# A four-layer graph network on one core: set-up work becomes steps in the ordered list of group steps, and split signals become whole ones

## What is computed

```python
h = relu(layernorm(x)); x = x + L0(h, adj)   # attention whose softmax runs over rows, plus h @ self_weight
h = relu(layernorm(x)); x = x + L1(h, adj)   # GAT, layernorm, relu, sum over (adj + (1+eps) I), MLP with a layernorm
h = relu(layernorm(x)); x = x + L2(h, adj)   # GAT with elu
h = relu(layernorm(x)); x = x + L3(h, adj)   # learned matrix A: off-diagonal and diagonal parts, two weights
...
def L1(x, adj):
    h = x @ Wp + bp
    scores = leaky_relu(s_src[:, :, None] + s_dst[:, None, :])
    attn = softmax(where(adj > 0, scores, fill), axis=-1)
    h_gat = relu(layernorm((attn * adj) @ h, gat_g, gat_b))
    z = relu(layernorm(((1 + eps) * h_gat + adj @ h_gat) @ W1 + b1, mlp_g, mlp_b))
    return relu(z @ W2 + b2 + h_gat)
...
def L3(x, adj, W, e, bias):        # e: values of the nonzero entries, in order of rows
    A = softmax(where(adj > 0, e[rank of the entry], NEG), axis=1)
    return (A off its diagonal) @ (x @ W[1]) + (its diagonal) * (x @ W[0]) + bias
```

## Time and profile before

| | |
|---|---|
| median of 3 runs | 968.9 us (968.21 to 969.45) |
| the profiled execution | 968.08 us, of which its span 966.3 us |
| PE busy | 906.3 us (94%) |
| PE weight loads busy | 857.2 us (89%) |
| DVE busy | 833.4 us (86%) |
| ACT busy | 757.8 us (78%) |
| POOL busy | 426.2 us (44%) |
| mean granted TensorE clock | 0.987 |

### The profile page before, as it was taken

How to read it: one execution, slowest core, us unless ns; L and a number is a source line. 1 busy time by engine, 2 the same in 40 slices (tenths; PEclk the granted TensorE clock), 3 DMA queues, 4 the chain that set the end, 5 groups by cost and what they waited for, 6 DMA issues and landing times. The chain is left out here.

```text
span 966.3 us, 21073 instructions
## 1 busy us (share of the span) xinstructions
PE 906.3 (94%) x7027; PEld 857.2 (89%) x7027; DVE 833.4 (86%) x2593; ACT 757.8 (78%) x2048; POOL 426.2 (44%) x1123
## 2 busy tenths in 40 slices
PE   4868899999998899999999999999999999998998
PEld 4668798999898899999989989989999999988997
DVE  5779899999869989988889989789999879789983
ACT  4698768877778887796887788898768787679953
POOL 6553326533546533362643454644353445244330
PEclk9889999999999999999999999999999999999999
DMA  5200000000020010011000101100100100000003
GB/s 139 66 2 2 2 2 1 1 2 1 23 65 3 1 45 1 2 44 45 1 2 1 45 2 45 44 2 1 45 1 2 46 1 2 22 2 1 1 2 110
DMA packets 43052, 20.05 MB, mean 21 GB/s; under 512 B 8248, under 2 KB 42432, under 8 KB 42944
## 3 DMA queue, kind: packets, MB, share of 16 engines
q1 hardware_dynamic: 41056, 18.49, 7.1%
q10 hardware_dynamic: 1888, 0.21, 0.2%
HBM read 10.17 MB, written 8.39 MB: 19 GB/s over the span
## 5 line engine op out<-in xcount | busy, mean ns | idle before, releaser
L729 PE MATMUL ps<-HE,PT 128*128 128x129 f32 x2048 | 239.4, 276 | 6.8 <-issue 4.4
L729 PEld LDWEIGHTS ps<-HE,PT 128*128 128x128 f32 x2048 | 233.2, 192 | 9.7 <-issue 6.7
L498 ACT ACTIVATE Y<-X,SM 128x128 f32<-128x128 f32 x512 | 204.1, 491 | 19.5 <-POOL SM L494 18.9
L479 POOL TENSOR_TENSOR SM<-ST 128x8 f32<-128x8 f32 x96 | 26.0, 271 | 380.5 <-DVE ST L1300 380.5
L1444 DVE SCALAR_TENSOR_TENSOR PT<-ps,CE,maskT 128x512 f32<-128x512 f32 x256 | 174.2, 743 | 16.8 <-PE ps L849 12.6
L490 POOL TENSOR_TENSOR SM<-SM,minus_half 128x8 f32<-128x8 f32 x96 | 163.6, 1704 | 7.6
L729 PE MATMUL ps<-W,HT 128*128 128x128 f32 x768 | 117.1, 275 | 0.1
L729 PEld LDWEIGHTS ps<-W,HT 128*128 128x128 f32 x768 | 106.1, 192 | 4.0 <-issue 0.7
L1300 DVE BATCH_NORM_STATS2 ST<-X 128x6 f32<-128x128 f32 x512 | 105.0, 278 | 3.4
L1075 ACT ACTIVATE HE<-ps,HE 128x128 f32<-128x128 f32 x256 | 68.9, 379 | 0.0
L748 PE MATMUL ps<-ident,Y 128*128 128x128 f32 x512 | 67.9, 276 | 1.0 <-ACT Y L498 0.6
(11 more groups left out here) (263 smaller groups left out, 2274.5 us busy)
## 6 DMA issues: line engine op xcount, KB each, us to landing
X<-in_x_dram SPq DMA_DIRECT2D x32, 256.0 KB, 3.5
out_dram<-X SPq DMA_DIRECT2D x32, 256.0 KB, 2.7
adj_raw<-in_adj_dram SPq DMA_DIRECT2D x4, 256.0 KB, 3.7
UP<-US SPq DMA_DIRECT2D x64, 2.0 KB, 1.8
W<-in_L_gnn_W_dram SPq DMA_DIRECT2D x2, 64.0 KB, 3.9
W<-in_L_gnn_W_dram SPq DMA_DIRECT2D x1, 128.0 KB, 3.6
feat0w<-L_gnn_others_weight_dram ACTq DMA_DIRECT2D x1, 64.0 KB, 3.3
feat1w<-in_L_gnn_Wp_dram ACTq DMA_DIRECT2D x1, 64.0 KB, 3.7
```

The costliest lines, as they stand in the source:

```text
L479: TT(sm[:, S_DIF, :], st[:, :, 1], st[:, :, 4], ALU.subtract)
L498: a = nc.scalar.activation(dst[:, n, 0:F], src[:, n, 0:F], func, scale=SM[s][:, S_RSTD, n:n + 1], bias=SM[s][:, S_SHIFT, n:n + 1])
L729: return nc.tensor.matmul(o, w, m, start=start, stop=stop, skip_group_check=True)
```

## The change

The first block is gone. Its constants, loads, transposes, and the copies of `maskT` and of the turned weights stand at the top of each engine's stream in the one block that is left; the rest became steps of group "g": `counts`, `masks`, `vecs` (DVE), `offs` (PE, ACT), `rows_b` (ACT), `offc` (PE, DVE), `biases` (POOL). The meeting of all engines is replaced by waits inside the steps that need a result: `made["vec"]` in PE's `feat0` and ACT's `norm0` of the first three groups, `made["bias"]` in ACT's `norm0`, PE's `feat1` and DVE's `shift3`, `made["masks"]` in `coefp0`, `coefb0`, `self0`, `made["counts"]` in `coefb0`. `egin` and `elow` move to the end of the list.

The loads are dealt out anew: `adj` pieces 0 and 2 on SP's queue, 1 and 3 on ACT's, where they stand ahead of the three weight matrices (`TURNED`) and of the seven columns that are left in `WEIGHTS`; `VECTORS` shrink from eleven DMAs to seven and go to SP's queue. DVE makes `adjn` piece by piece, waits for all of `WEIGHTS`, and then goes on to `counts`.

`scaled` signals once after all eight rows; so do `split0`, `splitb0`, `low0`, `lowb0`. `agg0` finishes one tile after the other. `TURNS` and `HOMES` are new strings.

DVE now begins with `counts`, 0:`stat0`, `masks`, `vecs`, `offc`, `erow`, 1:`stat0`, 2:`stat0`, `eat`, 4:`stat0`, 0:`feat0`. PE: `offs`, `offc`, `erank`, `eoffm`, 0:`norm0`, `eedge`, 1:`norm0`, 0:`feat0`, 1:`feat0`, `ecover`, `evalue`, 2:`norm0`, 2:`feat0`, 0:`cmax0`, 4:`norm0`, 1:`cmax0`, 0:`coefb0`, 1:`coefb0`, `eturn`, 0:`agg0`. ACT: `offs`, `rows_b`, `erank`, 0:`scale0`, 1:`scale0`, `eedge`, 0:`norm0`, 1:`norm0`, 0:`feat0`, `eat`, 1:`feat0`, 2:`scale0`, `emask`, 2:`norm0`, 2:`feat0`, 4:`scale0`, 0:`cmax0`, `esoft`, 1:`cmax0`, `escale`, 0:`split0`, 0:`splitb0`. POOL: 0:`stat0`, 1:`stat0`, `biases`, `egin`, 2:`stat0`, 4:`stat0`. Up to 0:`agg0` PE had the same steps before in another order, but for 4:`feat0` where there is now 2:`feat0`.

At the end, PE has f:`att2a`, c:`norm3`, f:`att2b`, c:`agg3`, e:`norm3`, e:`agg3`, c:`feat3`, d:`feat3`, f:`norm3`, f:`agg3`, e:`feat3`, f:`feat3`, where it had f:`att2a`, f:`att2b`, d:`norm3`, c:`feat3`, e:`norm3`, d:`agg3`, e:`agg3`, d:`feat3`, f:`norm3`, f:`agg3`, e:`feat3`, f:`feat3`. DVE has f:`elu2b`, e:`low3`, b:`shift3`, e:`shift3`, f:`elu2`, f:`stat3`, b:`feat3`, f:`low3`, where it had f:`elu2b`, d:`shift3`, f:`elu2`, f:`stat3`, e:`low3`, e:`shift3`, b:`feat3`, f:`low3`.

```diff
 PREP = [
-    ("egin", 0, "act pool"),
+    ("counts", 0, "dve"),
+    ("masks", 0, "dve"),
+    ("vecs", 0, "dve"),
+    ("offs", 2, "pe act"),
+    ("rows_b", 0, "act"),
+    ("offc", 1, "pe dve"),
+    ("biases", 0, "pool"),
     ("erank", 4, "pe act"),
-    ("elow", 0, "pool"),
     ("erow", 0, "dve"),
     ("eoffm", 1, "pe"),
     ("eedge", 4, "pe act"),
@@ -123,37 +128,39 @@
     ("esoft", 0, "act dve"),
     ("escale", 0, "act dve"),
     ("eturn", 4, "pe act dve"),
+    ("egin", 0, "act pool"),
+    ("elow", 0, "pool"),
 ]
 TURNS = {
-    "pe": ("gggg0g0114040112g02033112540530020101010341211120450331221052043221313233020030301551041104041214425"
-           "1454225100550255112132232642642276736344662237333234734344364546846875678486656883377737857784784884"
-           "9595558559896569956a6a79799a699666966a97676aa5575777877a8a7a7b6baa68ab86ba77bb8798988a88ab88dbc9bcbd"
-           "9bbabcda8cd89c9ca899d9adcaa99aa9becebcadcceadebcceedb99dd9eddebeceecbefbbfebdfbbfdbffcaacfdffaffdfcf"
-           "cccecceccfdfdddeddefdfdebeeebfeeffefeffbccffdcededffef"),
...
-    "pool": ("gg014201530123401250310412530242165734623476835878465979a68967a57a6b897b8abc9da89cdabcedbe9cebdfafcd"
-           "fecfdefbefcdef"),
...
+    "pool": ("01gg2430510120g341250310412530221465374623647873858469579a6986a577a6b897b8abcd9a89cabdcedbe9bcedfafc"
+           "dfecfdefbefdcef"),
+    "sp": ("0234501123450617672883994aa5bb6c7dcd8ee9ffdbacef"),
 }
...
+    "act": ("ggg01g010g12g2240g1g004g131343505201010220g103451011030315041241201022311305052332000423123141115025"
...
+    "dve": ("g0gggg12g403g1g0g20151g02g001g0101031114320023041041201512201035223543101343342125040442123531500253"
...
-        NORMED = ["norm0a", "norm0", "norm1a", "norm1", "gat1", "mlpb1a", "mlpb1", "norm2a", "norm2", "whole3", "norm3"]
+        NORMED = ["norm0", "norm1", "gat1", "mlpb1", "norm2", "whole3", "norm3"]
...
-        SIDES = ((0, 1, 4, 5), (2, 3, 6, 7))
-        HIS = {"a0": 0, "b0": 2, "1": 4, "3": 5}
-        LOS = {"0": 0, "b0": 2, "1": 4, "3": 5}
-        NHI = 6
+        HIS = {"a0": 0, "b0": 1, "1": 2, "3": 3}
+        LOS = {"0": 0, "b0": 1, "1": 2, "3": 3}
...
+        TURNED = [(feat0w[:, 0:F], Wo_d), (feat1w[:, 0:F], Wp_d), (feat2w[:, 0:F], Wq_d)]
+        WEIGHTS = [(att0[:, 0:1], att0_d[0:P, :]), (att0[:, 1:2], att0_d[P:2 * P, :]),
...
-                for t in range(T):
-                    sp.dma_start(adj_raw[:, t, :], adj[t * P:(t + 1) * P, :]).then_inc(adj_loaded, 16)
+                for t in (0, 2):
+                    sp.dma_start(adj_raw[:, t, :], adj[t * P:(t + 1) * P, :]).then_inc(adj_loaded[t], 16)
                 for s in range(NS // 2):
+                    if s == NS // 2 - 1:
+                        for dst, src in VECTORS:
+                            sp.dma_start(dst, src).then_inc(loaded["vectors"], 16)
                     for b in range(G):
                         sp.dma_start(X[s][:, b::G, :],
                                      x.rearrange("b (t p) f -> b p t f", p=P)[s * G + b]).then_inc(x_loaded[s], 16)
                 for dst, src in REST:
...
                 def turn_rows(u, name, s):
+                    pe.wait_ge(sig["normed"][s], count(u.g, len(NORMED), nd_at[name]))
                     src = HE[s] if name == "norm3" else Y[s]
                     for b in range(G):
-                        part = name + "a" if b == 0 and name != "norm3" else name
-                        pe.wait_ge(sig["normed"][s], count(u.g, len(NORMED), nd_at[part]))
                         o, done = open_tile(u, name, s, b)
                         for t in range(T):
...
                 def agg0(u, s):
-                    tiles = []
-                    for side in range(2):
-                        pe.wait_ge(sig["lo"][s], count(u.g, NHI, LOS["0"] + side))
-                        for t in range(HALF):
-                            if side == 0:
-                                tiles.append(open_tile(u, "agg0", s, t))
-                            o, done = tiles[t]
+                    pe.wait_ge(sig["lo"][s], count(u.g, len(LOS), LOS["0"]))
+
+                    for t in range(HALF):
+                        o, done = open_tile(u, "agg0", s, t)
+                        for side in range(2):
                             c = side * G * F
                             parts = [(k, m) for k in (2 * side, 2 * side + 1) for m in (HI, LO)]
                             for n, (k, m) in enumerate(parts):
                                 mm = MM(o[:, c:c + G * F], maskT[:, k, t * P:(t + 1) * P],
-                                        m[s][:, at0(k), :], side == 0 and n == 0, n == len(parts) - 1)
-                            if side == 1:
-                                mm.then_inc(done, 1)
+                                        m[s][:, at0(k), :], n == 0, n == len(parts) - 1)
+                        mm.then_inc(done, 1)
 
                 def self0(u, s):
 
-                    pe.wait_ge(sig["lo"][s], count(u.g, NHI, LOS["b0"]))
...
+                for t in (1, 3):
+                    act.dma_start(adj_raw[:, t, :], adj[t * P:(t + 1) * P, :]).then_inc(adj_loaded[t], 16)
+                for dst, src in TURNED:
+                    act.dma_start(dst, src).then_inc(loaded["turned"], 16)
+                for dst, src in WEIGHTS:
+                    act.dma_start(dst, src).then_inc(loaded["weights"], 16)
+                act.wait_ge(made["WT_ps"], 1)
...
+                def offs(u, s):
+                    for n, dst in enumerate((off_b, rowtot_b)):
+                        o, read = filled(u, "offs", s, n)
+                        A(dst[:], o, ACT.Copy).then_inc(read, 1)
+
+                def rows_b(u, s):
+                    act.wait_ge(loaded["vectors"], 16 * len(VECTORS))
+                    act.wait_ge(made["pool"], POOL_SETUP)
+                    A(bhi[32:33], brow[32:33], ACT.Copy).then_inc(made["bhi"], 1)
+                    for p0 in (0, 32):
+                        A(pick[p0:p0 + 1, :], ones[p0:p0 + 1, :], ACT.Copy)
+                    for k, bias in enumerate((bias_p, bias_1, bias_2, bias_q)):
+                        a = A(bias[0:1, 0:F], brow[0:1, k, :], ACT.Copy)
+                    a.then_inc(made["bhi"], 1)
...
+                        if name == "norm0" and u.group < NS // 2:
+                            act.wait_ge(made["vec"], 1)
+                            act.wait_ge(made["bias"], 1)
...
                 def normalise(u, name, s, dst, src, func=ACT.Relu):
 
                     act.wait_ge(sig["rstd"][s], count(u.g, NLN, ln_at[name]))
-                    if name == "gat1":
-                        scaled(dst, src, s, func).then_inc(sig["normed"][s], 1)
-                        return
-                    for b in range(G):
-                        scaled(dst, src, s, func, range(b, TG, G)).then_inc(sig["normed"][s], 1)
+                    scaled(dst, src, s, func).then_inc(sig["normed"][s], 1)
...
+                def biases(u, s):
+                    pool.wait_ge(loaded["rest"], 16 * len(REST))
+                    link(TS(bias3[:], bias3[:], -1.0, None, ALU.add))
+                    pool.wait_ge(made["bhi"], 1)
+                    for k, bias in enumerate((bias_p, bias_1, bias_2, bias_q)):
+                        link(TT(bias[32:33, 0:F], brow[32:33, k, :], bhi[32:33, k, :].bitcast(F32), ALU.subtract))
+                    pool.wait_ge(made["bhi"], 2)
+                    for p0 in (0, 32):
+                        link(TS(bias_n[p0:p0 + 1, :], bias_q[p0:p0 + 1, 0:F].bitcast(F32), float(N), None, ALU.mult))
+                    pool.sem_inc(made["bias"], 1)
+
...
+                for t in range(T):
+                    dve.wait_ge(adj_loaded[t], 16)
+                    V.tensor_scalar(adjn[:, t, :], adj_raw[:, t, :], 0.0, None, ALU.is_gt).then_inc(made["adjn"], 1)
+                dve.wait_ge(made["pool"], POOL_IDENT)
+                dve.wait_ge(loaded["weights"], 16 * len(WEIGHTS))
+                V.tensor_tensor(asum[:], asd[:, 0:1], asd[:, 1:2], ALU.add)
+                V.tensor_scalar(bprep[:], ones[:], bpcol[:, 0:1], None, ALU.mult).then_inc(made["bprep"], 1)
+
+                def counts(u, s):
+                    dve.wait_ge(made["adjn"], T)
+                    link(V.reduce_sum(cnt_row[:], adjn[:].bitcast(F32), AX_X))
+                    V.tensor_scalar(norow[:], cnt_row[:], 0.0, 1.0 / N, ALU.is_equal, ALU.mult)
+                    for k in range(T):
+                        a = V.tensor_scalar(cntrep[:, k, :], ones[:], cnt_row[:, k:k + 1], None, ALU.mult)
+                    a.then_inc(made["counts"], 1)
+                    dve.wait_ge(made["pool"], POOL_SETUP)
+                    V.tensor_copy(m_row[:], m_int[:])
```

More of the change, by code:

```diff
@@ L239, in gnn_kernel @@
         share8 = sb("share8", [P, TG])
-        loaded = {n: sem("loaded_" + n) for n in ("weights", "vectors", "rest")}
-        adj_loaded = sem("adj_loaded")
```

(14 more changed lines are left out.)

401 lines of the change are left out of this document (179 added, 222 removed).

## The result

The changed kernel takes 973.9 us (median of 20 runs, 971.55 to 975.83) and the kernel before, beside it on the same chip, 970.5 us (20 runs, 968.13 to 975.14). The ratio is 1.0033, with a 95% interval of 1.0024 to 1.0043: slower by 3.2 us (0.0033 x 970.5).

What follows compares the result with a forecast made beforehand. PE's own pace was taken to bound the middle, a chain through DVE, POOL and ACT the first 70 us. Start 2.0, middle 1.0 and end 1.4 gave +4.4 us on 968.9: 973.3 us, range 962 to 981.

Steps and rivals of the forecast that it cites:

- The start: First 70 us: 0:`agg0` begins on PE at 70.6 instead of 68.59, +2.0 us (from -1.5 to +6).
- the whole `low0`: Ahead of 0:`agg0`: PE waits for all eight rows of `low0` instead of four, 1.1 us.
- the end of `row_of`: DVE in the start: `row_of` ends at 31.0 us, 2.5 later than before.
- Landing of the weights: Start: `WEIGHTS` land at 13.0 us (12.0 to 14.5), so DVE's reduction starts at 13.4 instead of 9.32.
- The new wait: Start: DVE stops for all `WEIGHTS` ahead of `counts`, all its work behind that; reduction 4.1 us late.
- `adj` over two queues: Loads in the start: dealing `adj` over two queues does not bring all four pieces sooner.
- Parts 2 and 3: Whole-step hand-overs and the new order in the middle, 160 to 900 us: together +1.0 us.
- the 20 to 24: Sign that the forecast is right: PE's idle time from 160 to 900 us is 20 to 24 us.
- The end: Last group's chain up to f:`norm3`: 1.0 + 2.4 - 2.0 = +1.4 us (0 to +3.4).
- Rival (c): Whole steps are felt: PE waits at one in eight of 64 hand-overs, 13 us, about 984 us; chance 0.18.
- Rival (a): The new order hides half of PE's waits in the middle, -10.7 us, 961.6 us; chance 0.27.
- Rival (b): The start gains what it costs, -1.5 us there: 969.8 us in all, no change; chance 0.15.

Runs made afterwards that it cites:

- e4: Changed kernel with hand-overs in halves again and the order of before behind PE's 4:`agg0` (163 us): 0.9992 of before, 968.7 us.
- e3: Changed kernel, whole hand-overs kept, with the order of before behind PE's 4:`agg0` (163 us): 1.0010 of before, 970.4 us.
- e10: e4 with DVE's wait for the weights, `asum` and `bprep` moved behind `cntrep`: 0.9968 of before, 967.3 us.
- e11: Changed kernel with the order of before behind PE's e:`top2` (897 us) to the end, on every engine: 1.0031 of before, 973.3 us.
- e9: The changed kernel itself, unaltered, run once more beside before: 1.0042 of before, 973.9 us.

## Why the prediction was right, and where not

The forecast was 973.3 us, and 973.9 was measured: slower, by 3.2 us where the sum had 4.4. The way was right; that the total came so near was luck. The start was forecast 3 us too dear and the middle 2 to 3 us too cheap, and the two misses cancel. The kernel before was also 1.6 us slower in its 20 runs than the 968.9 that the forecast started from, so the absolute times agree better than the differences do.

**The start: +2.0 forecast, -0.8 to -1.3 measured (e4, e3).** The measured values hold for the order up to 163 us; e4's interval ends at 1.0005, so +2.0 is out. (1.1 of the forecast was the whole `low0`, which neither difference holds; without it, +0.9.) The step that failed is the end of `row_of`, 31.0 against 27.75.
- Landing of the weights: 13.0 taken, and `asum` starts at 12.19. The two DMAs ahead of `bpcol` pushed its issue from 5.71 to 6.61 us, but it landed 5.5 us later and not 6.3. The low bound was the right one; the reduction began 0.9 us sooner than forecast, at 12.46 and not 13.4.
- DVE's durations: I used those of before as they stood. Before, `below` took 1.63 us and `row_ofT` 2.37:

```profile
22.30 1.63 DVE L1513 TENSOR_SCALAR below<-m_row,end_col 128x256 f32<-128x256 f32 x4
...
24.76 2.37 DVE L1518 SCALAR_TENSOR_TENSOR row_ofT<-m_row,off_col,below 128x256 fp32r<-128x256 f32 x4
```

  They ran beside POOL's `diagg` (21.19 to 23.51) and `gin`. In the changed kernel POOL is idle there (22.8 to 29.4), and they take 1.14 and 1.67 us: 1.2 us of the miss. A step that is moved changes the durations of its old neighbours too. Both instructions took 1.4 times as long beside POOL. The Trainium skill ("SBUF — State Buffer", section "Who interferes with whom") gives the rule that I had used for the end and not here; the trace agrees with it for `row_ofT`, which reads two tiles of SBUF. `below` reads one tile and a column and was slowed as much, which the rule as I used it doesn't cover.
- The rest, some 1.1 us, has the same look. Six small DVE instructions that stood beside POOL's bias rows and `diagg` before are shorter now: `empty` (the cast) 0.45 to 0.18 us, `share` 0.43 to 0.16, `feat0w` 0.36 to 0.20, `e_hi` 0.36 to 0.15, `e_lo` 0.27 to 0.16, `end_col` 0.46 to 0.16, together 1.3. One stall of 0.24 us stands against it.

The new wait did cost: 2.66 us at DVE, and about 2.3 us of time by e10, with a wide error. So "behind that wait stands everything" was right, and it was paid for by savings that I had put too low.

`adj` over two queues: the pieces did land sooner, against what I had made of the rule. The tile `adj_raw`, time from issue of its DMAs to landing, the changed kernel first, then before:

```profile
DMA to landing us min/median/max: 3.9/4.3/4.9
```

```profile
DMA to landing us min/median/max: 3.1/3.7/5.6
```

The last piece was issued at 1.2 us and landed at 6.1; before, it was issued at 2.2 and landed at 7.8. 0.9 us of this is the earlier issue. The Trainium skill ("DMA: Bandwidth & Descriptors", section "Issuing engines are not separate DMA queues") says that issuing from several engines saves just that. The other 0.7 us is a shorter way from issue to landing (4.9 us, before 5.6); its cause is open. It won nothing: `adjn` was complete at 9.53, before at 9.28 (the reduction follows it at 9.32). DVE now made the first two pieces beside two long instructions of POOL and took 1.96 and 2.13 us for them, where the last piece took 0.41:

```profile
L1225 DVE TENSOR_SCALAR adjn<-adj_raw x4: 407/1284/2129, 4.7 to 9.1; 128x512 fp32r<-128x512 f32 x4
...
4.42 1.92 POOL L1141 TENSOR_SCALAR_AFFINE_SELECT upper<-work 128x2048 fp32r<-128x2048 f32 x1
6.29 2.10 POOL L1143 TENSOR_SCALAR_AFFINE_SELECT strict<-work 128x2048 fp32r<-128x2048 f32 x1
```

(The first line gives the shortest, median and longest of the four in ns.)

ACT's 0:`norm0` began at 37.50, not 41.0, as POOL's bias rows ended at 37.3 and not 40.7. From there to 0:`agg0` I had 29.6 us and it took 31.1. ACT's pauses there, which I took at 1.5 us, add up to 2.2; the other 0.8 us I can't place. PE waited 3.33 and 2.46 us in that stretch, the first time at a whole-step hand-over of norm rows. So 0:`agg0` came out at 68.60 and not 70.6. ACT's pause ahead of 1:`scale0` was 4.4 us, not 8.

**Parts 2 and 3: +1.0 forecast, 2.9 to 4.0 measured.** The change stands 0.0041 above e4 (1.0033 against 0.9992), 4.0 us. That is whole steps, the new order behind 163 us and the end together, where the sum had 2.4; with 0 to 1.1 for the end (e11), 2.9 to 4.0 are left. With the start's, this is the term that was mis-sized most. PE's pauses in the middle grew by 2.3 us in the changed trace (2.2 in e9's, 0.7 in e11's), inside the 20 to 24 that I named. The step that failed is the price of a felt hand-over. I read who waited in the trace of before, where halves hid the waits, and the earlier trace rows spoke of norm rows alone. The split rows, whose whole wait (the earlier trace rows gives it half of 2.21 us) I counted in the start only, stand in every group too; at 6:`agg0` they made the longest wait of the middle, 2.12 us, in two of the five traces that have whole split rows in the new order. And no term of the middle had the clock: there the pause was followed by 1.1 us that PE lost at half clock.

**The end: +1.4 forecast, 0 to 1.1 measured (e11).** POOL's long instruction went from 2.25 to 0.21 us, as forecast, with the two DVE operations out of its way: they now stand ahead of `elu2` (936.00 and 937.14). f:`norm3` has no pause ahead of it, where I had 1 to 3 us: PE had `agg3` and `feat3` of other groups to do until it came.

Rival (c) had the right mechanism at four to seven times its size (13 us against 1.8 to 3.0). Rival (a) is out: the new order was slower with whole steps and no faster with halves. Rival (b), an even start, was nearest to what the start did.

## What to carry to other kernels

Before a hand-over in halves is merged into one, list every group's copies of that hand-over, and price it in the new order, not by the waits of the old one: the halves are the reason why no wait shows. When a step is moved, take the durations of its neighbours from rows without it. A new wait early in an engine's list is worth moving behind the work that doesn't need it, even when the change around it looks even: here it gave some 2.3 us, with an error of 1.7.
